# A grouped convolution as 32x32 tiles of the array in f32, four groups at a time

## What is computed

```python
x = x + L0(gn(x), p1, p3, p4, p5, p6)
x = x + L1(gn(x), conv_w, gamma, beta)

def L0(x, p1, p3, p4, p5, p6):                       # n=16, c=128, h=w=32
    t1 = einsum('nchw,he->ncew', x, p1)              # h 32 -> e 16
    t2 = three row shifts of x, stacked
    t3 = conv(t1, p3, 9x9, padding 4, one filter per channel)
    t4 = conv(t3, p4, 5x1, padding 2, groups of 4 channels)
    t5 = einsum('ncew,ewf->ncf', t4, p5)             # f = 3c = 384
    t6 = conv(t5, p6, 1x3, one filter per channel)
    return einsum('ncf,nfp->ncp', t6, t2) / sqrt(3c)

def L1(x, conv_w, gamma, beta):
    # Haar details of x, upsampled, beside x: 512 channels; 1x1 convolution to 128;
    # batch normalisation over all images and pixels, gamma, beta, relu
```

## Time and profile before

| | us |
|---|---|
| median of 3 timed runs | 337.6 (336.77 to 340.73) |
| the profiled execution | 340.3 |
| its span, first to last instruction | 338.6 |

### The profile page before, as it was taken

One profiled execution on the slowest core, in us unless ns is written; L12 is line 12 of the kernel. 1 busy time (PEld: TensorE's weight loads), 2 busy tenths in 40 slices (PEclk: granted clock), 3 DMA queues, 4 the chain that ended last, 5 costly groups with the idle time before them and its releaser, 6 DMA issues.

```text
span 338.6 us, 4816 instructions
## 1 busy us (share of the span) xinstructions
PE 274.2 (81%) x1544; PEld 227.8 (67%) x1544; DVE 278.7 (82%) x539; ACT 231.7 (68%) x353; POOL 207.5 (61%) x203
## 2 busy tenths in 40 slices
PE   2565589998989998998999999999999998871000
PEld 0010079988889985777899898888999987751000
DVE  2899967898759798677789999999999999756992
ACT  0787728874858756736757878777778778555991
POOL 7497765691026945204888888888988888833000
PEclk9989759997979999999999999999999999998555
DMA  7999645677757484695000000000000000000699
GB/s 197 294 292 264 229 162 166 187 193 219 200 168 216 131 241 111 236 414 223 2 0 3 0 1 2 0 0 2 0 4 0 1 2 0 0 0 1 248 383 360
DMA packets 15257, 43.59 MB, mean 129 GB/s; under 512 B 3089, under 2 KB 3313, under 8 KB 15233
## 3 DMA queue, kind: packets, MB, share of 16 engines
q1 hardware_dynamic: 12832, 36.83, 33.4%
q10 hardware_dynamic: 1344, 4.20, 4.5%
q0 software_dynamic: 1056, 2.27, 2.4%
HBM read 30.44 MB, written 8.39 MB: 115 GB/s over the span
## 4 chain that ended last, share of the span: by engine, by line
PE 57%; DVE 13%; DMA 8%; ACT 7%; POOL 6%; issue 4%; SPq 3%; DVEq 0%; POOLq 0%; ACTq 0%
PE wide L723 12%; PE wide L247 9%; PE wide L249 8%; PE wide L248 8%; DMA x_slot<-in_x 7%; DVE x_sb L1070 5%; PE bank L800 4%; PE bank L247 4%; PE bank L249 3%; PE bank L248 3%; SPq L281 2%; PE bank L804 2%; DVE d_split L873 2%; DVE s_lo L864 2%; ACT s_hi L521 2%
## 5 line engine op out<-in xcount | busy, mean ns | idle before, releaser
L723 PE MATMUL wide<-t_all,s_hi 128*128 128x272 f32 (+1 forms) x320 | 47.8, 299 | 2.8 <-ACT t_all L512 1.6
L723 PEld LDWEIGHTS wide<-t_all,s_hi 128*128 128x128 f32 x320 | 44.2, 203 | 4.6 <-ACT t_all L512 3.1
L480 POOL TENSOR_TENSOR g_lo<-y_sb,g_hi 128x1024 fp32r<-128x1024 f32 x15 | 36.1, 2409 | 14.4 <-ACT y_sb L650 14.4
L456 POOL TENSOR_TENSOR g_lo<-y_sb,g_hi 128x1024 fp32r<-128x1024 f32 x15 | 35.9, 2396 | 12.0 <-ACT g_hi L610 12.0
L247 PE MATMUL wide<-g_hi,t_hi 128*128 128x512 f32 x96 | 37.5, 390 | 0.3 <-DVE t_lo L990 0.3
L858 DVE STREAM_TRANSPOSE xa<-x_slot 128x1024 f32<-128x1024 f32 x16 | 31.3, 2010 | 7.8 <-DMA x_slot<-in_x 7.2
L249 PE MATMUL wide<-g_hi,t_lo 128*128 128x512 f32 x96 | 37.5, 391 | 0.0
L248 PE MATMUL wide<-g_lo,t_hi 128*128 128x512 f32 x96 | 37.4, 390 | 0.0
L649 ACT ACTIVATE g_hi<-x_sb,rs 128x1024 fp32r<-128x1024 f32 x16 | 21.2, 1327 | 19.9 <-POOL rs L465 19.9
L864 DVE TENSOR_TENSOR s_lo<-s_f,s_hi 128x768 fp32r<-128x768 f32 (+1 forms) x32 | 26.2, 818 | 10.0 <-ACT s_hi L521 9.6
L402 POOL TENSOR_TENSOR t_all<-t_f,t_all 128x512 fp32r<-128x512 f32 x17 | 26.1, 1562 | 10.4 <-ACT t_f L515 10.4
(11 more groups left out here) (134 smaller groups left out, 832.7 us busy)
## 6 DMA issues: line engine op xcount, KB each, us to landing
s_f<-in_taps SPq DMA_DIRECT2D x32, 384.0 KB, 4.0
x_sb<-in_x SPq DMA_DIRECT2D x8, 1024.0 KB, 7.6
out<-x_sb SPq DMA_DIRECT2D x6, 1024.0 KB, 4.9
x_slot<-in_x ACTq DMA_DIRECT2D x12, 256.0 KB, 15.5
x_slot<-in_x SPq DMA_DIRECT2D x12, 256.0 KB, 15.5
d_sb<-t_out POOLq DMA_DIRECT2D x24, 76.5 KB, 3.2
d_sb<-t_out SPq DMA_DIRECT2D x24, 76.5 KB, 3.0
out<-x_sb SPq DMA_DIRECT2D x3, 512.0 KB, 2.8
```

Of the source, the lines that this page charges most:

```text
L456: pool.tensor_tensor(g1_lo[:, W:W + HW], y_sb[:, n, :], g1_hi[:, W:W + HW].bitcast(F32), ALU.subtract).then_inc(s["g1_lo"], 1)
L480: pool.tensor_tensor(g2_lo[:, :], y_sb[:, n, :], g2_hi[:, :].bitcast(F32), ALU.subtract).then_inc(s["g2_lo"], 1)
L723: mm = pe.matmul(ps_t3[g % 2][:, j0 * NO:j1 * NO], weights[:, g % SR, 128 * t:128 * t + 128], t1_all[:, row + j0:row + j1, :].rearrange("p ...
```

## The change

- **x** is loaded once, by channel (partition c), in 16 transfers of 512 KB, and stays in SBUF; no reload. The blocks of the transpose are now b = c // 32, and a group is (b, r): channel c = 32 b + 4 r + ci.
- **t1** is one f32 array, no parts. Its product is two accumulating 128x128 products per image (one for each parity) instead of two of 64. ScalarE copies it once.
- **Convolution** in R = 8 rounds r, each with the B = 4 groups (b, r) at once. Partitions 32 b to 32 b + 31 hold parity and row of block b. A product is a 32x32 tile: weights at the partitions of block b, output at the partitions of channel ci in PSUM bank b. No splitting of taps or t3.
- **The 5x1 filter** (`mix_product`): for every block b, output channel co and part jl of the columns a 32x32 product over 68 columns. Its output stands in PSUM in d's layout, so no transfers between partitions follow: ScalarE reads two banks at a time into d's high part (`d_high`), VectorE one bank at a time into the low part (`d_low`).
- **Statistics** of x: four images by ScalarE (before: one), the rest by VectorE, aggregated at round 6. Their product `gst_mm` stands after the last convolution round, and the four VectorE operations that end in `gst` stand between the low parts of rounds 6 and 7. The warming products before t5 wait for `gst`.
- **p5's low part** is made by GpSimd (before: VectorE), p5 and w are loaded in round 3. GpSimd has no more work in t1, taps and d.
- The loop over the images and the last pass keep their instructions; only places in SBUF and PSUM change.

```diff
+R, B = 8, 4
+TCOLS, MCOLS = CI * TAPS * 2 * E, B * C
+ACT_STATS = {4: 0, 7: 1, 10: 2, 13: 3}
+EARLY, PER_QUAD = 8, 3
 ...
+            for r in range(2, R):                     # SP
+                sp.wait_ge(s["conv"], r - 1)
+                load_taps(r)
+                sp.wait_ge(s["d_mm"], 2 * (r - 1))
+                load_mix(r)
 ...
+            for r in range(R):                        # ScalarE
+                act.wait_ge(s["conv"], r + 1)
+                if r >= 2:
+                    act.wait_ge(s["d_mm"], 2 * (r - 1))
+                act.copy(t3_sb[:, r % 2, :, :], ps_t3[:, :, 0:J * NO]).then_inc(s["t3_ev"], 1)
+                if r >= 1:
+                    d_high(r - 1)
 ...
-                    mm = pe.matmul(ps_t1[i % 4][64 * v:64 * v + 64, :], p1_blk[:, :], rhs, start=True, stop=True)
+                    mm = pe.matmul(ps_t1[i % 4], p1_blk[:, v, :], rhs, start=(v == 0), stop=(v == 1))
 ...
+            def convolve(r):
+                pe.wait_ge(taps_sem[r % 2], 16 * (r // 2 + 1))
+                if r >= 1:
+                    pe.wait_ge(s["t3_ev"], r)
+                for t in TAP_ORDER:
+                    j0, j1 = (2 if t == 0 else 0), (J - 2 if t == TAPS - 1 else J)
+                    for ci in range(CI):
+                        row = (CI * r + ci) * JP + t
+                        w = (ci * TAPS + t) * 2 * E
+                        for b in range(B):
+                            q = slice(32 * b, 32 * b + 32)
+                            mm = pe.matmul(ps_t3[32 * ci:32 * ci + 32, b, j0 * NO:j1 * NO],
+                                           taps[q, r % 2, w:w + 2 * E],
+                                           t1_all[q, row + j0:row + j1, :].rearrange("p j n -> p (j n)"),
+                                           start=(t == MID), stop=(t == TAP_ORDER[-1]))
+                mm.then_inc(s["conv"], 1)
+
+            def mix_product(r):
+                pe.wait_ge(mix_sem[r % 2], 16 * (r // 2 + 1))
+                pe.wait_ge(s["t3_ev"], r + 1)
+                ...
+                for h in range(2):
+                    if r >= 1:
+                        pe.wait_ge(s["d_lo"], B * (r - 1) + 2 * h + 2)
+                    for b in (2 * h, 2 * h + 1):
+                        for co in range(CI):
+                            w = (b * CI + co) * 2 * E
+                            for jl in range(JL):
+                                mm = pe.matmul(ps_d[32 * jl:32 * jl + 32, b, n * co:n * co + n],
+                                               mix[:, r % 2, w:w + 2 * E], t3_sb[:, r % 2, b, n * jl:n * jl + n],
+                                               start=True, stop=True)
+                    mm.then_inc(s["d_mm"], 1)
 ...
+            for r in range(R):
+                convolve(r)
+                if r >= 1:
+                    mix_product(r - 1)
+            pe.wait_ge(s["t3_ev"], R)
+            pe.wait_ge(s["st1"], 1)
+            pe.wait_ge(s["const"], 2)
+            pe.matmul(low[:, 0:2 * N], g_mean ..., mv1 ...).then_inc(s["gst_mm"], 1)
+            mix_product(R - 1)
 ...
-            pe.wait_ge(x_in[0], 16 * CI + 16)
-            keep_clock(WARM, ps_t6)
+            pe.wait_ge(x_in[0], 16)
+            pe.wait_ge(s["gst"], 1)
+            keep_clock(WARM, ps_y)
 ...
+            for r in range(R):                        # VectorE
+                ...                                   # three half images of statistics
+                if r >= 1:
+                    d_low(r - 1)
+            dve.wait_ge(s["gst_mm"], 1)
+            ...                                       # four operations on the statistics: gst
+            d_low(R - 1)
```

More of the change, by code:

```diff
@@ L50, with build @@
 STORES = [(0, 1), (1, 2), (2, 3), (3, 4), (4, 5)] + [(n, min(n + 2, N + 1)) for n in range(5, N + 1, 2)]
[L51 to L71, removed]
+TCOLS, MCOLS = CI * TAPS * 2 * E, B * C
+ACT_STATS = {4: 0, 7: 1, 10: 2, 13: 3}
+BY_ACT = len(ACT_STATS)
+EARLY, PER_QUAD = 8, 3
+AGGR_AT, ST1_AT, GST_AT = 6, 6, 7
+P5_RAW_AT, P5_AT, W_DET_AT = 3, 5, 6
+def build(nc, x, p1_blk_in, taps_in, mix_in, p5_in, p6, w_in, gamma, beta, out):
     ctx = ExitStack()
@@ L166, in build @@
[L166 to L170, removed]
+        taps = put("taps", [2, TCOLS])
+        mix = put("mix", [2, MCOLS])
+        t3_sb = put("t3_sb", [2, B, J * NO])
         assert cursor[0] <= nc.sbuf_top
         cursor[0] = end_d
-        g1_hi = put("g1_hi", [(H + 2) * W], F32R)
-        g1_lo = put("g1_lo", [(H + 2) * W], F32R)
@@ L204, in build @@
-        wide = [ctx.enter_context(nc.psum_tensor(f"wide{i}", [128, 1024], F32)) for i in range(2)]
+        low = ctx.enter_context(nc.psum_tensor("low", [128, 2048], F32))
+        high = ctx.enter_context(nc.psum_tensor("high", [128, 2048], F32))
+        bank = [high[:, 512 * i:512 * i + 512] for i in range(4)]
+        wide = [low[:, 1024 * i:1024 * i + 1024] for i in range(2)]
         ps_t1 = bank
-        ps_t3 = [wide[0][:, 0:J * NO], wide[0][:, 512:512 + J * NO]]
-        ps_t4 = [wide[1][:, 0:J * NO], wide[1][:, 512:512 + J * NO]]
+        ps_t3 = low[:, :].rearrange("p (b k) -> p b k", b=B)
@@ L324, in _, with load_taps, load_mix @@
-            load_taps(sp, 2)
+            def load_taps(r):
+                sp.dma_start(taps[:, r % 2, :], taps_in[r]).then_inc(taps_sem[r % 2], 16)
+            def load_mix(r):
+                sp.dma_start(mix[:, r % 2, :], mix_in[r]).then_inc(mix_sem[r % 2], 16)
+            load_x(sp, 0)
+            sp.dma_start(p1_blk[:, :, :], p1_blk_in).then_inc(s["p1_in"], 16)
+            for n in range(2, N, 2):
+                load_x(sp, n)
+                if n == N - 4:
+                    load_taps(0)
@@ new lines, in _, with d_high @@
+            for i in range(NO):
+                t1_copy(i)
+                if i in ACT_STATS:
+                    x_moments(ACT_STATS[i])
+            def d_high(r):
+                for h in range(2):
+                    act.wait_ge(s["d_mm"], 2 * r + h + 1)
+                    if r == 0 and h == 0:
+                        act.wait_ge(s["act_stats"], 2 * BY_ACT)
+                    src, hi, _ = d_views(r, slice(2 * h, 2 * h + 2))
+                    act.copy(hi, src).then_inc(s["d_hi"], 1)
@@ new lines, in _ @@
+            for r in range(R):
[5 more added lines that the diff above has]
+                    d_high(r - 1)
+                if r == P5_AT:
+                    act.wait_ge(s["p5_raw"], 16)
+                    for jc in range(JC):
+                        act.copy(p5_hi[:, jc, :], p5_raw[:, jc, :]).then_inc(s["p5_hi"], 1)
+                if r == W_DET_AT:
@@ L736, in _ @@
-            t4_product(G - 1)
+            for r in range(R):
[5 more added lines that the diff above has]
+            pe.wait_ge(s["const"], 2)
+            pe.matmul(low[:, 0:2 * N], g_mean[:, :, :].rearrange("p a b -> p (a b)"),
+                      mv1[:, :, :].rearrange("p n a -> p (n a)"), start=True, stop=True
+                      ).then_inc(s["gst_mm"], 1)
@@ L925, in _ @@
             last.then_inc(s["rs1"], 1)
-            for b in (NB - 2, NB - 1):
-                for piece in range(CI):
-                    d_low(b, piece)
             def u_views(k):
```

474 lines of the change are left out of this document (116 added, 358 removed).

## The result

The changed kernel takes 325.0 us (median of 4 runs, 322.79 to 325.89) beside 337.4 for the kernel before on the same chip (median of 4, 336.77 to 340.73). The ratio is 0.960, with a 95% interval of 0.952 to 0.968: faster, by 12.4 us. The forecast was 295, a gain of 42. The profiled execution took 325.89 for its span of 324.2.

What follows compares the result with a forecast made beforehand. TensorE was taken to bound the convolution at 5.2 us a round (2.8 + 2.4); t5 starts at 92.9 instead of 138.0, so 338.6 - 45.1 = 293.5, plus 1.7 gives 295 us. Range for 8 in 10: 285 to 326.

Steps and rivals of the forecast that it cites:

- the case that was forecast: Case A, the whole kernel: 295 us, its own range 285 to 302, chance 0.55.
- rival B: Convolution: faster but less so, by eight-tile overlap, an unhidden cost per pair or half clock; 302 to 328 us, chance 0.25.
- start of the convolution: End of the first stage: the convolution starts at 40.7 us, 3.8 earlier than before.
- 80 products: Convolution tile products of a round on 32x32 tiles: 2.8 us, with 16 tiles at once; bounds 2.2 and 18.2.
- short products: The 64 products of 68 columns in a round, four tiles at a time: 2.4 us a round.
- issue: TensorE's instruction supply in the convolution: 288 pairs a round at some 20 ns a pair, adding nothing to the sum.
- first copy of t3: ScalarE's copy before the first short products, which has no cover: 1.3 us.
- end of the last round: Behind round 6's short products: d's high half 1.2, two low parts 1.5, semaphores, then four small VectorE operations; 3.9 us.
- clock-keeping products: Twelve products ahead of t5, now waiting for the statistics: 7.7 us, 4.6 of them exposed after d is whole.
- Rival B's second form: Convolution: each pair has a cost other tiles do not hide; at 28 ns, 317 us; within B's 0.25.
- C (four tiles): Convolution: only four tiles work at a time, 9.1 us a round for the 80 products; 345 us, chance 0.06.
- D (strict order): Convolution: matmuls start in program order, second passes hold up other tiles; 18.2 us a round, 427 us, chance 0.14.

## Why the prediction was right in direction and wrong in size

**Direction and range held; the size did not.** And the range held by 1 us: 325.0 lies far outside the 285 to 302 of the case that was forecast, in rival B's share, just under the upper end of the range, 326. One round took 8.8 us (the products of rounds 1 and 7 start at 50.65 and 103.34), where 5.2 were forecast and 7 or more was named as B's sign; the granted clock was under 1.00 only between 70 and 80. The forecast for the start of t5 was 92.9; it was 123.9. The chain of waits divides these 31.0 us fully.

| step | forecast | measured | difference |
|---|---|---|---|
| start of the convolution | 40.7 | 45.3 | + 4.6 |
| 80 products, 8 rounds | 22.4 | 31.6 | + 9.2 |
| short products, 7 rounds | 16.8 | 16.5 | - 0.3 |
| "issue" | 0 | 15.8 | + 15.8 |
| first copy of t3 | 1.3 | 1.3 | 0 |
| end of the last round | 3.9 | 5.4 | + 1.5 |
| clock-keeping products | 7.7 | 7.9 | + 0.2 |

- The rows of the products and of "issue" are one sum: what the products don't take, the pieces do, as the run with few columns shows.
- **The step that failed is "Issue".** It took two semaphore instructions of the earlier trace rows, 20 instructions apart and 0.2 us apart in time (starts that are given to 0.1 us), as the rate at which TensorE gets instructions, and so found 20 ns a pair. The work as forecast left 18 ns a pair, so even by its own reading 288 pairs needed 5.8 us a round and not 5.2; the sum put the term at nothing. And 20 ns is near the rate inside a block only: with few columns, 127 pairs took 1.9 us between two pieces, 15 ns each. Over many blocks a pair costs 3.9 / 128 = 30 ns, and 288 of them 8.8 us a round, where 5.2 were forecast. The kernel before could not show it: a convolution group has 18 pairs in 2.18 us, 121 ns each. Rival B's second form, 28 ns a pair that other tiles do not hide, gave 317; its price was right, its place (a cost of each pair) was not. Had the rule been known, the sum would have been 40.7 + 70.6 + 7.7 = 119.0 for t5 and 321 us.
- **The 80 products** were forecast at 2.8 us and took 31.6 / 8 = 3.95. This second miss cost nothing of its own: with far fewer columns the stage kept its 70 us. The Trainium skill, "TensorE: Matmul & The Clock Gate", section Measured speedup vs the span model, has 16 tiles at 10.6 times the speed of one, and the estimate worked out from it was 3.4; the trace, with 3.95, stands nearer to it than to the forecast.
- **The overlap of tiles** was right. All 16 work at once, and the second pass of a tile does not hold the other tiles up. At the start of a round 32 records, both passes of 16 products, begin within 0.5 us, each of them about 0.4 long. L532 in 58.4 to 58.9 (count, ns, first and last start):

```profile
L532 PE MATMUL low<-t_all,taps x32: 387/400/413, 58.4 to 58.8; 32*32 32x272 f32 x32
```

  Rivals C (four tiles) and D (strict order) are out: they needed 9.1 and 18.2 us a round.
- **The first stage** missed by 4.6. Two things weren't seen. t1's first two products ran at half the pace, since TensorE had done nothing before (the early products took 1.9 to 3.2 us off). And the second buffer of `xa` comes free only when the product two images back is done; with the forecast 2.0 us for transpose and product alike there was no slack for that (the third buffer gave another 3.2). The text named both under "what would show it" and priced neither.
- **ScalarE's and VectorE's terms** held: the copy of t3 1.07 (forecast 1.2), the high part 1.24 (1.2), the low part 0.80 (0.75). VectorE was not the bound, with 35.6 us to spare.
- **The end of the last round** was 1.5 longer: the last short products wait for all four low parts of round 6 (2.96), where two (1.5) were counted.
- **The exposed clock-keeping products** were right: the last low part of d starts at 118.3 and takes 0.8, so 123.9 - 119.1 = 4.8 us lay bare (forecast 4.6), and the run with four of them gave 4.1 back.
- **Nothing lost behind t5**: 200.3 us, forecast 200.6.

## What to carry to other kernels

When a change multiplies the instructions of an engine, count them and set them against a sustained rate, not against a short burst: here TensorE got 256 instructions in some 3.8 us on the mean, so 128 passes of small f32 products with their weight loads took no less, whatever their columns. Look for "issue" pieces in the chain of waits that recur after an equal number of records. Work that was put under a wait (clock-keeping products, a second buffer) has to be sized again when the wait ends earlier.

## What the runs showed of the hardware

- TensorE's instructions come in transfers of 16,384 bytes, 256 instructions; with the engine at work on short ones, a block took 3.80, 3.81 and 3.88 us in three kernels, from stop to stop. The Trainium skill, "TensorEngine Tiling (Array Packing)", section Instruction Overhead, has about 60 cycles of overhead for each matmul, 25 ns at 2.4 GHz as an estimate; the 30 ns a pair of the long run are not far from it, but the trace has 32 starts within 0.5 us, and TensorE idles for the rest of a block's time. So the two agree only by the numbers.
- Of a block's 3.8 us the transfer is 0.9 to 1.6; from its end to TensorE's next instruction it was 1.2 to 1.6, and from there to the next transfer's start 1.0 or more, in every run. What fills the last two, and why no more than one block is fetched ahead here, stays open: taking away most of the stage's loads changed the stage by about 2 us in 70, and no run changed the size of a block or where it comes from.
- After some 3 us without work ahead of t5 (115.2 to 118.4), the granted clock was 0.50 from 119.2 to 122.4; with four products in the gap it stayed at 1.00.
- At the start of a program the granted clock in the profile reads 1.00 while products take 1,057 ns instead of 592; the records' durations tell it, the clock row does not.
- ScalarE wrote a strided bf16 row of 512 in 2.7 us, an f32 one in 1.1.
